# A state-space mixer and a 4-bit FFN on one core: the first group's list written anew

## The chip, the cores and the metric

The kernel runs on one core of a Trainium2 chip. The metric is the time of one execution on the device, in microseconds (us). The core has TensorE (PE; PEld is its weight load), VectorE (DVE), ScalarE (ACT), GpSimd (POOL) and SyncE (SP), which here only issues transfers. Each has its own instruction stream, in program order, and they meet through semaphores.

## The reference

Input is `u`, 16 sequences of 256 tokens with 256 features (4096 tokens). Cut to what matters:

```
zxbcdt = u @ W_in                              # z 512, x 512, B 128, C 128, dt 8
xBC = silu(causal_conv4(xBC));  dt = softplus(dt + dt_bias);  A = -exp(A_log)
Y   = ssd(x * dt, A * dt, B, C) + x * D        # per sequence, 8 heads of 64
y   = rmsnorm(Y * silu(z)) * norm_scale @ W_out
h   = layernorm(u + y)
W   = dequant(4-bit codes, scales of 32)       # gate, up: 2048 x 256; down: 256 x 2048
out = layernorm(h + (gelu(h @ Wg.T) * (h @ Wu.T)) @ Wd.T)
```

All matmuls of weights are done three times over with operands that are split into a high and a low fp32r part.

## The kernel before

**Groups.** The 4096 tokens are cut into nine groups: FIRST (number -1, 256 tokens, two tiles of 128), groups 0 to 6 (512 tokens, four tiles each) and LAST (number 7, 256 tokens). In `run(g, ...)` the mixer of group g is interleaved with the FFN of group g-1; FIRST has no FFN beside it, and its FFN runs beside the mixer of group 0. The order on every engine is a hand-written list, `SLOTS`, with names for steps: `x4`, `x5` (B and C channels), `x0` to `x3`, `z0` to `z3` (projection, convolution, silu), `CB0` (C·B products), `R0`, `R1` (decay exponents spread over 128 x 1024, ACT's part eight instructions of 128x128 into a high tile, DVE's one into a low tile), `D0`, `D1` (their prefix sums on PE, exp on ACT, product with `cb` on DVE), `XT` (transposes of x), `Y` (outputs), `g` (squares and the split of the gated output), `S` and `op` (mean square, output projection), `ln1`, `ln2` (layernorm). After the list come `uT` (split of the next group's transposed input into high, on ACT, and low, on POOL), `F1` (transposes of h into the banks `gate_bank` and `up_bank`), and `dt` and `x4` of the next group. Each step that needs a PSUM bank takes the next of four `mixer` banks by its place in `USES`.

**Weights.** The FFN's weights come as 8 packed blocks of codes (`packed`) and 24 chunks of scales. A chunk c (c%3: gate, up, down) is made in five steps: `decode(b)` on DVE (five instructions for a block of three chunks), `value(c)` on DVE (codes times scales into half of `h_res`, or into `act_sb` for odd c from 12), `upper(c)` on ACT (high part), and then for the first 12 chunks "take off" on PE (two matmuls that leave value minus high part in one of the banks `gate_bank`, `up_bank`, `down0`, `down1`) and `lower(c)` on ACT; for the others `rest(c)` on DVE. The tables `DECODE`, `VALUE`, `UPPER`, `TAKE_OFF`, `LOWER` say behind which step of the list each stands. `value(c)` waits until the take-off of chunk c-2 is done, the take-off of c for the lower part of c-4, since they share buffers.

**SP's queue.** SP issues all loads in one order, and waits in that order. Ahead of the scales of chunk c it waits until `value(c-2)` is done; ahead of the scales of chunk 3k it waits until k+1 blocks are decoded and then loads the next block; ahead of the scales of chunk 14 it does this:

```python
                if c == BESIDE_FIRST + 2:
                    load_uT(0)

                    sp.wait_ge(wt_lo.sem, BESIDE_FIRST)
                    keep_h(FIRST)
                    load_u(0)
```

`BESIDE_FIRST` is 12 and `wt_lo` counts finished lower parts. `load_uT(0)` waits for the last use of `xbc` in FIRST's `Y1`; `keep_h` copies h from `h_sb` to `h_res` once h is there; `load_u(0)` waits for that copy.

Of the kernel before, what the change touches and what calls it, by code (L numbers as in the profile page):

```python
# [13 lines left out]
P = 128  # L14
# [39 lines left out]
DECODE = {FIRST: {"x1": [2], "XT0": [3], "g0": [4]}, 0: {"x5": [5], "x1": [6], "x3": [7]}}  # L54
VALUE = {FIRST: {"x0": [2], "x1": [3], "x2": [4], "x3": [5], "D0": [6], "XT0": [7], "XT1": [8], "Y1": [9],
                 "g0": [10], "op0": [11]},
         0: {0: [12], "x0": [13], 1: [14], "z1": [15], "x2": [16], 3: [17], "z3": [18], "CB0": [19], 5: [20],
             6: [21], "XT1": [22], "D1": [23]}}
UPPER = {FIRST: {"x1": [2], "z0": [3], "z1": [4], "CB0": [5], "D1": [6], "Y0": [7], "Y1": [8], "g0": [9],
                 "op0": [10], "g1": [11]},  # L60
         0: {"x0": [12], "z0": [13], "x1": [14], 2: [15], "z2": [16], "x3": [17], 4: [18], "XT0": [19], "D0": [20],
             "Y0": [21], 7: [22], 8: [23]}}
TAKE_OFF = {"x5": [0], "x0": [1], "z0": [2], "x2": [3], "x3": [4], "D0": [5], "Y0": [6], "XT1": [7],
            "g0": [8], "op0": [9], "g1": [10], "op1": [11]}
LOWER = {FIRST: {"x1": [0], "z0": [1], "z1": [2], "x3": [3], "CB0": [4], "D1": [5], "XT1": [6], "Y1": [7],
                 "op0": [8], "g1": [9], "op1": [10], "ln1": [11]},
         0: {"z0": [12], "x1": [13], 2: [14], "z2": [15], "x3": [16], 4: [17], "XT0": [18], "D0": [19], "Y0": [20],
             7: [21], 8: [22], "XT2": [23]}}
# [49 lines left out]
def mamba_ffn_kernel(nc, u, u_t, W_in, channels, dt_bias, A_log, W_out, ffn_w, ffn_s, out):  # L118
# [42 lines left out]
    with ExitStack() as ctx:  # L161
# [60 lines left out]
        R_first = [x[:, :, :].rearrange("p k (h l) -> p (k h) l", l=P) for x in (hT_hi, hT_lo)]  # L222
# [3 lines left out]
        def R_of(g):  # L226
            return R_first if kind_of(g) == "first" else (R_hi, R_lo)
# [103 lines left out]
        def wait_R(eng, i, g):  # L331

            if i:
                wait_ready(eng, f"D{i - 1}b" if i % 2 else f"E{i // 2 - 1}", g)
            elif kind_of(g) != "first":
                wait_ready(eng, "z3", g)
            wait(eng, dA_ok, g, 1)
# [11 lines left out]
        def run(g, mixer, ffn, prep=None):  # L349


            first = kind_of(g) == "first"
# [10 lines left out]
            if not last:  # L363
# [125 lines left out]
        def _(pe):  # L489
# [18 lines left out]
            def mixer(name, g):  # L508
# [35 lines left out]
                elif kind == "D":  # L544
# [3 lines left out]
                    for n, use in enumerate((f"D{i}a", f"D{i}b")):  # L548
                        wait_bank(pe, use, g)
                        hs = slice(4 * n, 4 * n + 4)  # L550
                        upper, lower = R_of(g)
                        nc.tensor.matmul(bank(g, use)[:, :], after_r[:, :], upper[:, hs, :], start=True, stop=False)  # L552
                        nc.tensor.matmul(bank(g, use)[:, :], after_r[:, :], lower[:, hs, :], start=False,
                                         stop=True).then_inc(ready(g, use)[0].sem, 1)
                    if i % 2:
# [4 lines left out]
                        for a, rows in ((1, P), (0, HP)):  # L560
                            for n, part in enumerate(R_of(g)):
# [86 lines left out]
            def prep(g, item):  # L648
                for c in TAKE_OFF.get(item, ()) if kind_of(g) == "first" else ():
# [29 lines left out]
        def _(act):  # L679
# [134 lines left out]
            act.wait_ge(x_in.sem, 16)  # L814
            nc.scalar.activation(win_hi[:, :, X0:B0], x_raw, ACT.Copy).then_inc(win_top.sem, 1)
            upper(0)
            act.wait_ge(z_in.sem, 16)
            nc.scalar.activation(win_hi[:, :, 0:X0], z_raw, ACT.Copy).then_inc(win_top.sem, 1)
# [4 lines left out]
            upper(1)  # L823
# [4 lines left out]
        def _(dve):  # L828
# [275 lines left out]
            def prep(g, item):  # L1104
                for c in LOWER[g].get(item, ()) if kind_of(g) != "first" else ():
# [143 lines left out]
```

## Time and profile before

| | |
|---|---|
| median of 3 runs | 955.6 us (955.42 to 955.68) |
| the profiled execution's own time | 955.01 us |
| span of its trace | 953.3 us |
| PE busy | 892.7 us (94%) |
| DVE busy | 704.9 us (74%) |
| ACT busy | 532.2 us (56%) |

The span is what the trace covers; all times of single instructions below count from its start. Busy time is a union of an engine's instructions, and PE's is modelled in part. In the trace, FIRST's `F1` begins at 74.41 us and that of group 0 at 178.12 us.

### The profile page before, as it was taken

What the parts mean: (1) busy time and instruction counts of PE and PEld (TensorE: products, weight loads), DVE (VectorE), ACT (ScalarE), POOL (GpSimd) and SP (SyncE); (2) the same over time, 40 slices, a digit from 0 to 9 for tenths busy, and PEclk for the clock granted to TensorE, in tenths of its full rate; (3) what the DMA queues carried; (4) which work ended last, traced back from release to release, by engine and by line L of the source; (5) the groups of instructions that cost most, each with busy time, mean ns of one, the idle gap of its engine ahead of it and who ended that gap; (6) DMA issues with size and microseconds to landing.
All of it is one profiled execution on the core that took longest, in us unless ns stands there. A gap on an engine that the chain in (4) does not pass through costs nothing.

```text
span 953.3 us, 16507 instructions
## 1 busy us (share of the span) xinstructions
PE 892.7 (94%) x5632; PEld 773.0 (81%) x5632; DVE 704.9 (74%) x1566; ACT 532.2 (56%) x1016; POOL 72.3 (8%) x104
## 2 busy tenths in 40 slices
PE   4777789899999999999999999999999999999997
PEld 3446678788898888888888888888888888888887
DVE  6767988787769776786779876786779776867453
ACT  4743486448645775448735674547635674456232
POOL 2101000200011000200020000200020000200000
PEclk9787899999999999999999999999999999999999
DMA  4111100010002000010001000010002000100010
GB/s 135 33 58 49 32 18 12 23 45 1 1 23 67 0 0 22 22 44 0 0 22 66 0 0 22 31 35 0 0 22 67 1 1 13 45 12 1 1 35 12
DMA packets 18651, 23.13 MB, mean 24 GB/s; under 512 B 1584, under 2 KB 15152, under 8 KB 18608
## 3 DMA queue, kind: packets, MB, share of 16 engines
q1 hardware_dynamic: 18176, 22.56, 7.4%
q8 instruction: 24, 0.39, 0.2%
q14 instruction: 19, 0.16, 0.1%
q10 hardware_dynamic: 432, 0.03, 0.0%
HBM read 14.19 MB, written 4.19 MB: 19 GB/s over the span
## 4 chain that ended last, share of the span: by engine, by line
PE 78%; DVE 10%; issue 6%; POOL 3%; ACT 2%; DMA 1%; POOLq 0%; DVEq 0%; SPq 0%; ACTq 0%
PE gate_bank L493 6%; PE up_bank L493 6%; PE up_bank L495 6%; PE up_bank L494 6%; PE gate_bank L495 5%; PE gate_bank L494 5%; PE down L493 5%; PE down L495 5%; PE mixer L493 5%; PE down L494 5%; PE mixer L495 5%; PE mixer L494 5%; PE mixer L573 3%; DVE xbc L904 2%; PE mixer L552 2%
## 5 line engine op out<-in xcount | busy, mean ns | idle before, releaser
L493 PE MATMUL down<-wd_hi,in_hi 128*128 128x256 f32 x512 | 145.1, 283 | 0.7 <-DVE in_lo L1035 0.7
L495 PE MATMUL down<-wd_hi,in_lo 128*128 128x256 f32 x512 | 144.0, 281 | 0.0
L494 PE MATMUL down<-wd_lo,in_hi 128*128 128x256 f32 x512 | 143.8, 281 | 0.0
L904 DVE SCALAR_TENSOR_TENSOR xbc<-mixer,chan,xbc 128x510 f32<-128x510 f32 (+1 forms) x162 | 110.9, 685 | 27.8 <-ACT xbc L703 26.1
L760 ACT ACTIVATE in_hi<-act_sb 128x512 fp32r<-128x512 f32 (+1 forms) x144 | 83.4, 579 | 65.3 <-PE down L495 53.7
L1049 DVE SCALAR_TENSOR_TENSOR act_sb<-up_bank,act_sb 128x512 f32<-128x512 f32 (+1 forms) x144 | 90.4, 628 | 37.5 <-PE up_bank L495 18.5
L774 ACT ACTIVATE act_sb<-gate_bank 128x512 f32<-128x512 f32 (+1 forms) x144 | 79.0, 548 | 67.7 <-PE gate_bank L495 67.0
L493 PE MATMUL gate_bank<-hT_hi,wg_hi 128*128 128x512 f32 (+1 forms) x288 | 111.4, 387 | 3.1 <-DVE wg_lo L1102 3.1
L493 PE MATMUL up_bank<-hT_hi,wu_hi 128*128 128x512 f32 (+1 forms) x288 | 108.4, 376 | 6.4 <-DVE act_sb L1049 6.4
L495 PE MATMUL up_bank<-hT_hi,wu_lo 128*128 128x512 f32 (+1 forms) x288 | 107.8, 374 | 0.0
L494 PE MATMUL up_bank<-hT_lo,wu_hi 128*128 128x512 f32 (+1 forms) x288 | 107.8, 374 | 0.0
L495 PE MATMUL gate_bank<-hT_hi,wg_lo 128*128 128x512 f32 (+1 forms) x288 | 107.1, 372 | 0.0
L494 PE MATMUL gate_bank<-hT_lo,wg_hi 128*128 128x512 f32 (+1 forms) x288 | 107.0, 371 | 0.0
L1035 DVE TENSOR_TENSOR in_lo<-act_sb,in_hi 128x512 fp32r<-128x512 f32 (+1 forms) x144 | 90.0, 625 | 20.7 <-ACT in_hi L760 20.7
L493 PEld LDWEIGHTS down<-wd_hi,in_hi 128*128 128x128 f32 x512 | 97.3, 190 | 5.6 <-DVE in_lo L1035 1.1
L494 PEld LDWEIGHTS down<-wd_lo,in_hi 128*128 128x128 f32 x512 | 97.2, 190 | 4.5
L703 ACT ACTIVATE xbc<-mixer,chan 128x512 f32<-128x512 f32 (+1 forms) x54 | 39.4, 729 | 107.2 <-PE mixer L495 107.2
L495 PEld LDWEIGHTS down<-wd_hi,in_lo 128*128 128x128 f32 x512 | 97.1, 190 | 0.0
L493 PE MATMUL mixer<-uT_hi,win_hi 128*128 128x512 f32 (+1 forms) x180 | 71.2, 395 | 12.4 <-DVE wdt L1126 11.4
L1159 POOL TENSOR_TENSOR rms<-rms_v,minus_half 128x1 f32<-128x1 f32 x32 | 20.1, 628 | 741.4 <-DVE rms_v L991 741.4
L728 ACT ACTIVATE uT_hi<-tri,dA_hi 128x128 fp32r<-128x128 f32 x240 | 73.2, 391 | 0.0
L493 PEld LDWEIGHTS up_bank<-hT_hi,wu_hi 128*128 128x128 f32 x288 | 55.2, 192 | 18.3 <-DVE act_sb L1049 8.0
(200 smaller groups left out, 1936.2 us busy)
## 6 DMA issues: line engine op xcount, KB each, us to landing
xbc<-in_u_t_dram SPq DMA_DIRECT2D x7, 512.0 KB, 3.6
h_sb<-in_u_dram SPq DMA_DIRECT2D x7, 512.0 KB, 3.8
h_res<-h_sb SPq DMA_DIRECT2D x7, 512.0 KB, 2.9
out_dram<-h_res SPq DMA_DIRECT2D x7, 512.0 KB, 2.9
scales<-in_ffn_s_dram SPq DMA_DIRECT2D x24, 128.0 KB, 2.1
packed<-in_ffn_w_dram SPq DMA_DIRECT2D x8, 96.0 KB, 2.1
xbc<-in_u_t_dram SPq DMA_DIRECT2D x2, 256.0 KB, 2.8
xbc<-in_W_in_dram SPq DMA_DIRECT2D x1, 512.0 KB, 6.2
```

Source lines behind the costliest of these rows:

```text
L493: nc.tensor.matmul(dst, lh, rh, start=first, stop=False, skip_group_check=True)
L494: nc.tensor.matmul(dst, lh, rl, start=False, stop=False, skip_group_check=True)
L495: return nc.tensor.matmul(dst, ll, rh, start=False, stop=last, skip_group_check=True)
L573: mm = nc.tensor.matmul(bank(g, use)[a * HP:(a + 1) * HP, j * P:(j + 1) * P], xdt[:, h * HP:(h + 1) * HP], dec_of(g, i)[:, h, :], start=Tr ...
L703: nc.scalar.activation(xbc[:, i, 0:width(g)], bank(g, f"x{i}")[:, 0:width(g)], ACT.Identity, bias=chan[:, 24 + i:25 + i], scale=chan[:, 18 ...
L728: ins = nc.scalar.activation(R_of(g)[0][:, h, :], tri[:, :], ACT.Copy, scale=f32(dA_hi[:, i, h:h + 1]))
L760: nc.scalar.activation(in_hi[:, n % 2, 0:width(f)], act_sb[:, n % 2, 0:width(f)], ACT.Copy)\
L774: nc.scalar.activation(act_sb[:, n % 2, 0:width(f)], GB[:, 0:width(f)], ACT.Gelu_apprx_tanh, scale=CODE_SCALE).then_inc(gelu_ok.sem, 1)
L904: ins = stt(acc[:, :, d:], src[:, :, 0:SEQ - d], chan[:, c:c + 1], acc[:, :, d:], ALU.mult, ALU.add)
L1035: tt(in_lo[at], act_sb[at], f32(in_hi[at]), ALU.subtract)\
L1049: stt(inter, UB[:, 0:width(f)], CODE_SCALE, inter, ALU.mult, ALU.mult)\
L1159: tt(rms[:, i:i + 1], rms_v[:, i:i + 1], half[:, 0:1], ALU.pow).then_inc(rms_ok.sem, 1)
```

## The change

Six things change, all before the FFN of group 0 begins.

1. SP loads the B, C and dt columns of `W_in` second, ahead of the first packed block and of the x columns, and z's columns ahead of packed block 1.
2. DVE splits those columns before it decodes block 0; chunks 0 and 1 get their values later, and `x4` of FIRST starts before the x columns are split.
3. FIRST's list has `CB0` behind `x0`, `R0` behind `x1` and `R1` behind `x2`. So both R pairs exist at once, and `R1` lies in a part of `wd_hi`, `wd_lo` that is not yet filled.
4. `D` is parted: `D` is what PE and ACT do, `W` DVE's product with `cb`. `g0` stands ahead of `Y1`.
5. The tables place the chunks anew. Blocks 1 to 4 are decoded behind `z3`, `XT1`, `S1`, `ln2`. The take-offs of chunks 10 and 11 move to `x5` and `x0` of group 0, `F1` of FIRST waits for ten lower parts, not twelve, and the first `down` for eleven.
6. `uT` of group 0 stands in FIRST's list behind `S1`, and SP loads it ahead of the scales of chunk 7 instead of 14.

The full groups' order on each engine stays as it was (`W` directly behind `D`).

```diff
-    "first": [["x5", "x0", "x1", "z0", "x2", "z1", "x3", "z2", "z3", "CB0", "R0", "D0", "R1", "XT0", "D1", "Y0",
-               "XT1", "Y1", "g0", "S0", "op0", "g1", "S1", "op1", "ln1", "ln2"], []],
+    "first": [["x5", "x0", "CB0", "x1", "R0", "z0", "x2", "z1", "R1", "x3", "z2", "z3", "D0", "XT0", "D1", "W0", "W1",
+               "Y0", "XT1", "g0", "Y1", "S0", "op0", "g1", "S1", "uT", "op1", "ln1", "ln2"], []],
...
-DECODE = {FIRST: {"x1": [2], "XT0": [3], "g0": [4]}, 0: {"x5": [5], "x1": [6], "x3": [7]}}
+DECODE = {FIRST: {"z3": [1], "XT1": [2], "S1": [3], "ln2": [4]}, 0: {"x5": [5], "x1": [6], "x3": [7]}}
...
             sp.dma_start(u32[:, :, 0:HALF], uT_of(FIRST)).then_inc(uT_in.sem, 16)
+            sp.dma_start(bc_raw, win_v[:, :, B0:NIN]).then_inc(bc_in.sem, 16)
             load_block(0)
-            sp.dma_start(bc_raw, win_v[:, :, B0:NIN]).then_inc(bc_in.sem, 16)
+            sp.dma_start(x_raw, win_v[:, :, X0:B0]).then_inc(x_in.sem, 16)
             load_scales(0)
-            sp.dma_start(x_raw, win_v[:, :, X0:B0]).then_inc(x_in.sem, 16)
-            load_block(1)
             load_scales(1)
             sp.dma_start(z_raw, win_v[:, :, 0:X0]).then_inc(z_in.sem, 16)
+            load_block(1)
...
             for c in range(2, CHUNKS):
+                if c == 7:
+                    load_uT(0)
                 if c == BESIDE_FIRST + 2:
-                    load_uT(0)
...
-                        pe.wait_ge(wt_lo.sem, BESIDE_FIRST)
+                        pe.wait_ge(wt_lo.sem, BESIDE_FIRST - 2)
```

The names below are the program's tiles; `codes` and `packed` are decoding, `h_res<-codes,scales` is a `value`, `dec` and `act_sb` with `cb` are the `W` products.

SP's queue from chunk 2's scales to chunk 14's, first before, where `uT` of group 0, `keep_h` and `load_u` stand together:

```order
L415 DMA scales<-in_ffn_s_dram 128x256
L410 DMA packed<-in_ffn_w_dram 128x192
L415 DMA scales<-in_ffn_s_dram 128x256 x3
L410 DMA packed<-in_ffn_w_dram 128x192
L415 DMA scales<-in_ffn_s_dram 128x256 x2
L441 DMA xbc<-in_u_t_dram 128x2x512
L450 DMA h_res<-h_sb 128x512
L455 DMA h_sb<-in_u_dram 128x4x256
L415 DMA scales<-in_ffn_s_dram 128x256
```

and the same end of it in the changed program:

```order
L420 DMA scales<-in_ffn_s_dram 128x256
L446 DMA xbc<-in_u_t_dram 128x2x512
L420 DMA scales<-in_ffn_s_dram 128x256 x2
L415 DMA packed<-in_ffn_w_dram 128x192
L420 DMA scales<-in_ffn_s_dram 128x256 x3
L415 DMA packed<-in_ffn_w_dram 128x192
L420 DMA scales<-in_ffn_s_dram 128x256 x2
L455 DMA h_res<-h_sb 128x512
L460 DMA h_sb<-in_u_dram 128x4x256
L420 DMA scales<-in_ffn_s_dram 128x256
```

`keep_h` and `load_u` keep their place ahead of chunk 14's scales (the last row of both), and the load of `uT` has gone up.

DVE in FIRST from `z3` on, before (`cb`, `R0`, product 0, value 5, `R1`, `XT0`):

```order
L925 SCALAR_TENSOR_TENSOR zs<-zs,mixer 128x256
L931 TENSOR_TENSOR cb<-mixer,tri 128x128
L932 TENSOR_TENSOR cb<-mixer,tri 128x128
L935 TENSOR_TENSOR hT_lo<-tri,dA_lo 128x1024
L948 COPY tail<-dec 128x8
L953 TENSOR_TENSOR dec<-dec,cb 128x1024
L1094 TENSOR_TENSOR h_res<-codes,scales 128x512
L935 TENSOR_TENSOR hT_lo<-tri,dA_lo 128x1024
L940 TENSOR_TENSOR xdt<-mixer,dt_sb 128x512
```

and after, where the second row is the first of block 1's decoding and the `h_res` row is `value(3)`:

```order
L934 SCALAR_TENSOR_TENSOR zs<-zs,mixer 128x256
L1079 TENSOR_SCALAR codes<-packed 128x192
L1081 SCALAR_TENSOR_TENSOR codes<-packed,codes 128x192
L1082 TENSOR_SCALAR codes<-packed 128x192
L1084 TENSOR_SCALAR packed<-packed 128x192
L1086 TENSOR_TENSOR codes<-packed,codes 128x192
L1100 TENSOR_TENSOR h_res<-codes,scales 128x512
L949 TENSOR_TENSOR xdt<-mixer,dt_sb 128x512
L955 COPY tail<-dec 128x8
L1015 TENSOR_TENSOR xtail<-xdt,tail 128x512
L959 TENSOR_TENSOR dec<-dec,cb 128x1024
L959 TENSOR_TENSOR act_sb<-act_sb,cb 128x1024
```

`cb` and both R have moved ahead of `z3`, and between `z3` and the products stand a decoding and a value.

ACT at the start of group 0 from FIRST's first `F1` copy on, before:

```order
L767 ACTIVATE hT_hi<-gate_bank 128x256
L767 ACTIVATE hT_hi<-up_bank 128x256
L703 ACTIVATE xbc<-mixer,chan 128x512
L708 ACTIVATE dte<-dte 128x32
L703 ACTIVATE xbc<-mixer,chan 128x512
L774 ACT_TABLE_LOAD
L774 ACTIVATE act_sb<-gate_bank 128x256
L703 ACTIVATE xbc<-mixer,chan 128x512
L687 ACTIVATE y<-xbc 128x512 x2
L781 ACTIVATE wg_hi<-h_res 128x2x256
```

and after, from the convolution copy of `x5` to the lower part of chunk 11 (`wd_hi` is upper 11, `wu_lo` lower 10, `wg_hi` upper 12, `wd_lo` lower 11):

```order
L712 ACTIVATE xbc<-mixer,chan 128x512
L790 ACTIVATE wd_hi<-h_res 128x512
L794 ACTIVATE wu_lo<-down 128x2x256
L783 ACT_TABLE_LOAD
L783 ACTIVATE act_sb<-gate_bank 128x256
L712 ACTIVATE xbc<-mixer,chan 128x512
L696 ACTIVATE y<-xbc 128x512 x2
L790 ACTIVATE wg_hi<-h_res 128x2x256
L794 ACTIVATE wd_lo<-down 128x512
```

Upper 11 and lower 10 stand ahead of the table load now. The twelfth lower part, on which `keep_h` waits, has moved from FIRST to behind upper 12.

## Rows read from the trace of the kernel before

**Rows 1.** Busy time by stretch: busy (instructions) per engine, PEclk, DMA share, GB/s.

```profile
0.00:74.90 74.90, 44.92 (x208) 31.54 (x209) 53.45 (x131) 38.38 (x83) 12.90 (x26) 0.86 0.24 72
74.90:140.00 65.10, 53.23 (x312) 46.54 (x311) 55.55 (x123) 38.52 (x82) 0.00 (x0) 0.84 0.12 36
...
80.00:85.00 5.00, 5.00 (x18) 4.42 (x19) 3.41 (x7) 1.78 (x3) 0.00 (x0) 0.50 0.33 103
```

**Rows 2.** Timeline of the start: start us, us, engine, line, operation [idle before <-releaser].

```profile
1.81 0.43 SPq L419 DMA_DIRECT2D y<-in_W_in_dram  x1
...
7.39 0.63 ACT L812 ACTIVATE win_hi<-y 128x512 fp32r<-128x512 f32 x1 [2.79 <-DMA y<-in_W_in_dram]
...
10.35 0.68 DVE L1123 TENSOR_TENSOR win_lo<-y,win_hi 128x512 fp32r<-128x512 f32 x1
...
11.38 0.55 PE L493 MATMUL mixer<-uT_hi,win_hi 128*128 128x256 f32 x1 [11.38 <-DVE wdt L1126]
```

**Rows 3.** Timeline of DVE: the silus of `x4`, `x5` in FIRST; a decoding's first row, the row behind.

```profile
22.30 0.75 DVE L839 SCALAR_TENSOR_TENSOR xbc<-y,xbc 128x256 f32<-128x256 f32 x2
...
47.81 0.25 DVE L1073 TENSOR_SCALAR codes<-packed 128x192 int32<-128x192 int32 x1
...
49.23 1.22 DVE L953 TENSOR_TENSOR act_sb<-act_sb,cb 128x1024 f32<-128x1024 f32 x1
```

**Rows 4.** Timeline of ACT in FIRST: W_out's scaling, and `R0`.

```profile
23.14 1.69 ACT L800 ACTIVATE zs<-zs,chan 128x256 f32<-128x256 f32 x4
...
37.57 2.43 ACT L728 ACTIVATE hT_hi<-tri,dA_hi 128x128 fp32r<-128x128 f32 x8
```

**Rows 5.** The page: transfers, KB each, median us from issue to landing.

```profile
h_sb<-in_u_dram SPq DMA_DIRECT2D x7, 512.0 KB, 3.8
...
scales<-in_ffn_s_dram SPq DMA_DIRECT2D x24, 128.0 KB, 2.1
...
h_res<-h_sb SPq DMA_DIRECT2D x2, 256.0 KB, 3.2
...
y<-in_W_in_dram SPq DMA_DIRECT2D x1, 264.0 KB, 5.6
```

**Rows 6.** Timeline of PE: a take-off and the next one, and FIRST's `F1`.

```profile
62.94 1.91 PE L655 MATMUL up_bank<-h_res,ident 128*128 128x512 f32 x2
...
65.07 1.06 PE L655 MATMUL down<-h_res,ident 128*128 128x512 f32 x2
...
74.41 0.50 PE L626 MATMUL gate_bank<-ident,h_sb 128*128 128x128 f32 x2 [4.14 <-DVE h_sb L1029]
```

**Rows 7.** Timeline of DVE: the normalization of h at FIRST's end, and that line over the run.

```profile
71.80 2.54 DVE L1029 TENSOR_SCALAR h_sb<-h_sb,mv,lnr 128x256 f32<-128x256 f32 x2 [1.16 <-POOL lnr L1148]
...
L1029 DVE TENSOR_SCALAR h_sb<-h_sb,mv,lnr x32: 401/408/1354, 71.8 to 893.7; 128x256 f32<-128x256 f32 x32
```

**Rows 8.** Timeline, PE and DVE: `x4` of group 1, and DVE's first step on its dt.

```profile
181.17 0.41 PE L493 MATMUL mixer<-uT_hi,win_hi 128*128 128x512 f32 x1
...
184.46 0.19 DVE L855 TENSOR_TENSOR dtx<-mixer,dtb 128x32 f32<-128x32 f32 x1 [1.29 <-PE mixer L504]
```

**Rows 9.** Timeline of DVE in group 0: dt, `x5`'s convolution, value 12, value 14.

```profile
80.66 0.19 DVE L855 TENSOR_TENSOR dtx<-mixer,dtb 128x32 f32<-128x32 f32 x1 [4.55 <-PE mixer L504]
...
84.31 2.31 DVE L904 SCALAR_TENSOR_TENSOR xbc<-mixer,chan,xbc 128x510 f32<-128x510 f32 x3 [0.79 <-ACT xbc L703]
...
88.42 0.68 DVE L1094 TENSOR_TENSOR h_res<-codes,scales 128x512 f32<-128x512 fp8e4 x1
...
95.21 0.68 DVE L1094 TENSOR_TENSOR h_res<-codes,scales 128x512 f32<-128x512 fp8e4 x1
```

**Rows 10.** Timeline of SP's queue: `keep_h`, `load_u`, and the scales of chunk 14.

```profile
74.43 0.53 SPq L450 DMA_DIRECT2D h_res<-h_sb  x1
78.67 0.39 SPq L455 DMA_DIRECT2D h_sb<-in_u_dram  x1
89.13 0.34 SPq L415 DMA_DIRECT2D scales<-in_ffn_s_dram  x1
```

More of the change, by code:

```diff
@@ L38 @@
 SLOTS = {
[3 rows of a table removed]
[3 rows of a table added]
              ["S3", "op3", "ln1"], ["ln2"]],
[4 rows of a table removed]
[4 rows of a table added]
+             [], [], []]}
 BESIDE_FIRST = 12
-DECODE = {FIRST: {"x1": [2], "XT0": [3], "g0": [4]}, 0: {"x5": [5], "x1": [6], "x3": [7]}}
-VALUE = {FIRST: {"x0": [2], "x1": [3], "x2": [4], "x3": [5], "D0": [6], "XT0": [7], "XT1": [8], "Y1": [9],
-                 "g0": [10], "op0": [11]},
+DECODE = {FIRST: {"z3": [1], "XT1": [2], "S1": [3], "ln2": [4]}, 0: {"x5": [5], "x1": [6], "x3": [7]}}
+VALUE = {FIRST: {"x0": [1], "x2": [2], "D0": [3], "W1": [4], "g0": [5], "Y1": [6], "op0": [7], "g1": [8], "op1": [9],
+                 "ln1": [10], "ln2": [11]},
@@ L57 @@
          0: {0: [12], "x0": [13], 1: [14], "z1": [15], "x2": [16], 3: [17], "z3": [18], "CB0": [19], 5: [20],
[L58 to L68, printed above, removed]
+             6: [21], "XT1": [22], "W1": [23]}}
+UPPER = {FIRST: {"CB0": [1], "z1": [2], "D1": [3], "Y0": [4], "g0": [5], "g1": [6, 7], "S1": [8], "ln1": [9],
+                 "ln2": [10]},
+         0: {"x5": [11], "x0": [12], "z0": [13], "x1": [14], 2: [15], "z2": [16], "x3": [17], 4: [18], "XT0": [19],
+             "D0": [20], "Y0": [21], 7: [22], 8: [23]}}
@@ new lines @@
+TAKE_OFF = {FIRST: {"x5": [0], "x1": [1], "x3": [2], "W1": [3], "XT1": [4], "Y1": [5], "S1": [6], "op1": [7, 8],
+                    "ln1": [9]},
+            0: {"x5": [10], "x0": [11]}}
+LOWER = {FIRST: {"x0": [0], "z0": [1], "z2": [2], "g0": [3], "Y1": [4], "op0": [5], "op1": [6, 7], "ln1": [8],
+                 "ln2": [9]},
+         0: {"x5": [10], "x0": [11]}}
+REST = {"z0": [12], "x1": [13], 2: [14], "z2": [15], "x3": [16], 4: [17], "XT0": [18], "W0": [19], "Y0": [20],
+        7: [21], 8: [22], "XT2": [23]}
@@ L220, in mamba_ffn_kernel, with R_of @@
         wout_raw = zs[:, :, HALF:]
-        R_first = [x[:, :, :].rearrange("p k (h l) -> p (k h) l", l=P) for x in (hT_hi, hT_lo)]
+        R_first = [[x.rearrange("p k (h l) -> p (k h) l", l=P) for x in pair]
+                   for pair in ((hT_hi[:, :, :], hT_lo[:, :, :]), (wd_hi[:, 12:16, :], wd_lo[:, 12:16, :]))]
         dec_first = act_sb[:, :, :].rearrange("p k (h l) -> p (k h) l", l=P)
         minus_i = in_hi[:, 0, HALF:HALF + P]
-        def R_of(g):
-            return R_first if kind_of(g) == "first" else (R_hi, R_lo)
+        def R_of(g, i):
+            return R_first[i] if kind_of(g) == "first" else (R_hi, R_lo)
         def dec_of(g, i):
@@ L331, in wait_R @@
         def wait_R(eng, i, g):
[L333 to L336, printed above, removed]
+            if kind_of(g) != "first":
+                wait_ready(eng, f"D{i - 1}b" if i % 2 else f"E{i // 2 - 1}" if i else "z3", g)
             wait(eng, dA_ok, g, 1)
@@ L362, in run @@
             last = kind_of(g) == "last"
-            if not last:
+            if not first and not last:
                 mixer("uT", g + 1)
@@ L550, in mixer @@
                         hs = slice(4 * n, 4 * n + 4)
-                        upper, lower = R_of(g)
+                        upper, lower = R_of(g, i)
                         nc.tensor.matmul(bank(g, use)[:, :], after_r[:, :], upper[:, hs, :], start=True, stop=False)
@@ L560, in mixer @@
                         for a, rows in ((1, P), (0, HP)):
-                            for n, part in enumerate(R_of(g)):
+                            for n, part in enumerate(R_of(g, i)):
                                 mm = nc.tensor.matmul(bank(g, use)[0:rows, :],
@@ L648, in prep @@
             def prep(g, item):
-                for c in TAKE_OFF.get(item, ()) if kind_of(g) == "first" else ():
+                for c in TAKE_OFF[g].get(item, ()):
                     b = chunk_bank(c)
@@ L727, in mixer @@
                     for h in range(H):
-                        ins = nc.scalar.activation(R_of(g)[0][:, h, :], tri[:, :], ACT.Copy,
+                        ins = nc.scalar.activation(R_of(g, i)[0][:, h, :], tri[:, :], ACT.Copy,
                                                    scale=f32(dA_hi[:, i, h:h + 1]))
@@ L790, in prep @@
                     upper(c)
-                for c in LOWER[g].get(item, ()) if kind_of(g) == "first" else ():
+                for c in LOWER[g].get(item, ()):
                     lower(c)
@@ L796, in any_mixer @@
                 mixer(name, g)
+                if name == "x5" and kind_of(g) == "first":
+                    upper(0)
+                    act.wait_ge(z_in.sem, 16)
+                    nc.scalar.activation(win_hi[:, :, 0:X0], z_raw, ACT.Copy).then_inc(win_top.sem, 1)
                 if name == "x1" and kind_of(g) == "first":
@@ L813, in _ @@
             nc.scalar.activation(wdt[:, :, 0, :], bc_raw[:, :, DT0 - B0:], ACT.Copy).then_inc(win_top.sem, 1)
[L814 to L818, printed above, removed]
             act.wait_ge(small_in.sem, 16 * 2)
@@ L822, in _ @@
             mixer("x4", FIRST)
-            upper(1)
+            act.wait_ge(x_in.sem, 16)
+            nc.scalar.activation(win_hi[:, :, X0:B0], x_raw, ACT.Copy).then_inc(win_top.sem, 1)
             run_all(act, any_mixer, ffn, prep)
@@ L941, in mixer @@
                        dt_sb[:, i, :].unsqueeze(2).to_broadcast([P, H, HP]), ALU.mult).then_inc(x_ok.sem, 1)
-                    if kind_of(g) == "first" and i == 0:
-                        x_tail(i, g)
-                elif kind == "D":
+                elif kind == "W":
                     d = dec_of(g, i)
@@ L1104, in prep @@
             def prep(g, item):
-                for c in LOWER[g].get(item, ()) if kind_of(g) != "first" else ():
+                for c in REST.get(item, ()) if kind_of(g) != "first" else ():
                     rest(c)
@@ L1135, in _ @@
             mixer("x4", FIRST)
+            value(0)
+            dve.wait_ge(win_top.sem, 3)
+            tt(win_lo[:, :, X0:B0], x_raw, f32(win_hi[:, :, X0:B0]), ALU.subtract).then_inc(win_ok.sem, 1)
             run_all(dve, mixer, ffn, prep)
```

18 lines of the change are left out of this document (8 added, 10 removed), and 12 rows, old and new, of tables (SLOTS, USES).

## The prediction

> **What bounds the kernel now.** I read the busy time by stretch first. From 140 us on PE is the bound: of the page's 892.7 us the two first stretches hold 98.2 [rows 1], so the other 813 us of the span hold 794.6 of them, 98%. The change touches nothing there, so the time can only change by the moment at which PE comes to its dense part. Ahead of it lie FIRST (to 74.41 us, PE busy 44.9 of 74.9) and the first half of group 0, where DVE is busy 55.6 of 65.1 us and PE 53.2 [rows 1]. The timeline of DVE shows where that half has slack: 4.55 us before dt, 0.79 before `x5`'s convolution [rows 9], then almost none until 122 us. So a microsecond by which DVE is late between 90 and 122 us is a microsecond of the whole, and one by which it gets its dt earlier is one too. Two numbers decide: when FIRST's `F1` begins (74.41 [rows 6]), and how long DVE then takes to its dense part and through it.
>
> **FIRST, step by step.** Times are from the span's start; instructions whose rows are not shown are priced by the same timelines, at their distance from start to start.
>
> The B, C columns were issued at 1.81 and used at 7.39, a landing of 5.6 us [rows 2, 5]. They are issued 0.5 earlier and have no packed block ahead: I take 6.7 us, with 4.5 (a landing like the 3.2 us of a 256 KB copy [rows 5]) and 6.9 as bounds. From the landing PE's first matmul follows after 0.7 (ACT's copy 0.63) plus 1.03 (10.35 to 11.38, the two DVE splits [rows 2]), since value 0, value 1 and their scales no longer stand ahead. That is 8.4 instead of 11.38, 3.0 earlier.
>
> Of this most goes again. The silus of `x4` and `x5` began 10.9 us after PE's first matmul (11.38 to 22.30 [rows 2, 3]); now value 0 (0.6) and the x split (1.1) stand inside, and the silus take 0.75: 21.8. PE has `CB0` behind `x0` and waits for them, and behind it stands `x1`. PE has then been idle for some 4 us, and after such an idle (4.14 us before 74.41 [rows 6]) the granted clock was 0.50, the 1.2 GHz level, in 80 to 85 us [rows 1]; at that level `CB0` and `x1` cost 1.4 and 1.3: 24.5 instead of 20.2. From there ACT leads: copy and tanh (0.8), W_out (1.7 [rows 4] and 1.0), `R0` 2.4 [rows 4], z0's tanh, lower 1, `x2`'s copy (1.3): DVE's convolution of `x2` at 32.0, which began at 29.7. DVE's convolution, silu and value 2 (2.5), ACT's upper 2, `R1`, copy of `x3` (3.5): 38.0. Convolution, silus and z of `x3` (2.9): 40.9, where before z3 ended at 37.4. But `cb` and both R are made by then. They cost DVE 3.74 us of waiting for exp alone before.
>
> Decoding block 1 costs 1.4 (47.81 to 49.23 [rows 3]): 42.3. Here is a new wait: SP loads block 2 only when block 1 is decoded, and chunk 3's scales behind it, while `value(3)` is DVE's next instruction. Issue 0.4 and a landing of 2.1 to 2.3 [rows 5] make it 44.9 to 45.1. I found nothing that hides it; the transposed x and both products queue behind it. From 45.1 DVE's list runs to the end of `Y1` without a wait that I can find, 13.9 us: 59.0 (58.2 before). `g0` is then done, decoding 2 too.
>
> Next, `value(8)` waits for take-off 6, which stands behind `S1` on PE. `S1` can start at 63.5; a take-off costs 2.1 at the low level (62.94 to 65.07 [rows 6]) and 1.2 at the high one: `value(8)` at 64.7 to 66.0. Decoding 3 ends some 2.2 later, and chunk 9's scales wait behind packed block 4 as above: 2.5. Values 9, statistics and the power on POOL cost 2.9. The normalization itself gets cheaper: 2.54 us for two instructions beside POOL's split of `uT`, which is now done long before, against a median of 0.41 each otherwise [rows 7]: 0.8 for both, 1.8 saved. `F1` comes at 73.2 (takes at the high level) to 74.5; I take 74.0. The ten lower parts that it waits for are there by then. **First term: -0.4 us** (-2.4 to +0.5).
>
> **Group 0, the clock.** PE works almost without a gap from `S1` (63.5) on: take-offs 6 to 9 and `op1`, and waits under 2 us before `F1`, not 4.14 [rows 6]. With the low level (0.50 [rows 1]) `F1` to DVE's dt took 6.25 us (74.41 to 80.66 [rows 6, 9]); `x4` of group 1 to dt took 3.3 (181.17 to 184.46 [rows 8]), with `F1` 3.7. DVE is free 2.7 us after `F1` (value 11, decoding 4, split of h stand there now, hidden by its wait). So up to 2.5 from the first wait and 0.79 from the second [rows 9], 3.3 in all; in this group a gap of 1.9 us was followed by 3.4 us at the low level, which leaves 1.6; nothing if PE stays low. **Second term: -2.3 us** (-3.3 to 0). The two take-offs that moved here, ACT's three instructions (1.5 us) and the table load behind lower 10 are hidden: PE idles 12 us of this half and ACT 26 [rows 1], and DVE reaches the first product only after decoding 5.
>
> **Group 0, SP's queue.** `keep_h` was issued at 74.43, as soon as h was there, `load_u` 4.24 later, and chunk 14's scales at 89.13 when `value(12)` was done [rows 10]; `value(14)` did not wait for them. Now `keep_h` waits for the twelfth lower part, which ACT does behind upper 12, so behind `value(12)`: 1.1 after its end (upper and lower), up to 2.5 if the tanhs are late. From `value(12)`'s end (89.0) to `value(14)` (95.2) were 6.2 us [rows 9]. Against them stand 1.1 to 2.5, the copy, 4.24 [rows 10] or the 3.2 of its row [rows 5], 0.4 for `load_u`, and the scales' landing: 2.1 alone, up to 3.9 behind 512 KB that land in 3.8 [rows 5]. That is 6.8 to 11.0; `value(14)` waits for 0.6 to 4.8 us. I take 2.5: the copy between its prices, the scales between theirs, ACT on time. Queued behind `value(14)` are `x1`'s convolution and all of DVE, and behind upper 14 on ACT the gelu of unit 2, so PE's unit 3. DVE has no slack to give it back. **Third term: +2.5 us** (+0.6 to +4.8).
>
> The Trainium skill bears on this term ("DMA: Bandwidth & Descriptors", section "Anatomy of one DMA"): about 2.0 us fixed plus the bytes at 436 GB/s. By it the 256 KB copy would take 2.6 us and the scales 2.3, and the third term would be near +0.2, the sum 2.5 us below 955.6. Its copy and the trace's, 4.24, differ.
>
> **Sum.** -0.4 - 2.3 + 2.5 = -0.2 us on the profiled execution's 955.01, which lies 0.6 below the median: 955.4 for the median.
>
> **Rivals.** What can be told from no change is 0.2%, 1.9 us: below 953.7 or above 957.5.
>
> *The queue costs nothing* (0.16). Copy and scales land quickly, and `value(14)` waits 0.6. For it: the median of the two 256 KB copies, 3.2 [rows 5]. Against: 4.24 at this very place. -0.4 - 2.3 + 0.6 = -2.1: 953.5.
>
> The Trainium skill's rule above is the same case with 953.1.
>
> *B and C land early* (0.10), at 4.5: the chain of FIRST keeps 2.2 more. For it: nothing stands ahead but `uT`. Against: 5.6 us for rows of 1056 B. 953.2.
>
> *FIRST's waits are overrated* (0.07): high clock at its end and ACT's chain shorter. About 953.
>
> *PE stays at the low level into group 0* (0.13). The gap before `F1` or before `S1` drops it. For it: in 74 to 85 us it stayed low for over 10 us [rows 1, 6]. The second term is gone: 957.7. It decides once less than 0.2 us of the 2.3 are left.
>
> *The queue at its upper price* (0.13): 4.24, scales behind `load_u`, tanhs late, 4.8: 957.7.
>
> *The change does nothing* (0.03): all is absorbed before 122 us, 955.6. With my own forecast (0.38) this is the case of no change.
>
> **Numbers.** Faster 0.33 (0.16 + 0.10 + 0.07), same 0.41, slower 0.26. My own case ranges over 953.8 to 957.4. The range takes in the rivals of both sides and, since they can meet, a little beyond each: 952.0 to 958.7.
>
> **What would show it.** Right: PE's first matmul near 8.4; DVE waits some 2.5 us on scales before `value(3)` and again before `value(9)`; h's normalization 0.4 each; `F1` between 73 and 75; dt of group 0 3.7 to 5.5 us behind `F1`; SP issues `keep_h` some 16 us behind `F1`, and DVE waits for scales before `value(14)`. Wrong: `F1` below 72 or above 76; no wait before `value(14)`; a wait in group 0 that I don't name, above all of ACT behind lower 10.

## Result: 0.4% slower, outside the range

The changed kernel takes 959.27 us (median of 5, 957.37 to 961.87) against 955.6 for the kernel before in the same series, a ratio of 1.004 (95% interval 1.0022 to 1.0057). The forecast was 955.4, in a range up to 958.7. Sent again with the experiments it gave 959.47, ratio 1.0047 (1.0033 to 1.006). The execution profiled first is the fastest of its five, 957.37, with a span of 955.7; the later one took 959.74, span 957.9. Both are used, since they differ in FIRST.

The start of the changed kernel, by the timeline (columns as in [rows 2]):

```profile
1.31 0.46 SPq L423 DMA_DIRECT2D y<-in_W_in_dram  x1
...
5.82 0.63 ACT L825 ACTIVATE win_hi<-y 128x512 fp32r<-128x512 f32 x1 [1.27 <-DMA y<-in_W_in_dram]
...
7.51 0.55 PE L499 MATMUL mixer<-uT_hi,win_hi 128*128 128x256 f32 x1 [7.51 <-DVE wdt L1129]
```

The columns land in 4.5 us instead of 5.6, and PE begins 3.9 us sooner than in [rows 2]. Then DVE's timeline of the changed kernel, in order: values 3, 8 and 9, the normalization of h, dt of group 0, `x5`'s convolution, values 12 and 14.

```profile
45.52 0.69 DVE L1100 TENSOR_TENSOR h_res<-codes,scales 128x512 f32<-128x512 fp8e4 x1 [3.05 <-DMA scales<-in_ffn_s_dram]
...
66.38 0.69 DVE L1100 TENSOR_TENSOR h_res<-codes,scales 128x512 f32<-128x512 fp8e4 x1 [1.83 <-PE down L666]
...
71.16 0.69 DVE L1100 TENSOR_TENSOR h_res<-codes,scales 128x512 f32<-128x512 fp8e4 x1 [2.00 <-DMA scales<-in_ffn_s_dram]
...
74.38 0.74 DVE L1035 TENSOR_SCALAR h_sb<-h_sb,mv,lnr 128x256 f32<-128x256 f32 x2 [0.95 <-POOL lnr L1152]
...
82.11 0.19 DVE L864 TENSOR_TENSOR dtx<-mixer,dtb 128x32 f32<-128x32 f32 x1 [4.30 <-PE mixer L510]
...
85.75 2.31 DVE L913 SCALAR_TENSOR_TENSOR xbc<-mixer,chan,xbc 128x510 f32<-128x510 f32 x3 [0.79 <-ACT xbc L712]
...
89.86 0.68 DVE L1100 TENSOR_TENSOR h_res<-codes,scales 128x512 f32<-128x512 fp8e4 x1
...
98.49 0.69 DVE L1100 TENSOR_TENSOR h_res<-codes,scales 128x512 f32<-128x512 fp8e4 x1 [1.75 <-issue]
```

The brackets are the reading. The two waits for scales in FIRST stand where the queue was said to make them. But dt still waits 4.30 us for PE and `x5` 0.79, as in [rows 9]. FIRST's `F1` on PE, and SP's queue, in the changed kernel (to [rows 6, 10]):

```profile
75.18 0.70 PE L635 MATMUL gate_bank<-ident,h_sb 128*128 128x128 f32 x2 [1.92 <-DVE h_sb L1035]
...
91.92 0.53 SPq L455 DMA_DIRECT2D h_res<-h_sb  x1
94.27 0.39 SPq L460 DMA_DIRECT2D h_sb<-in_u_dram  x1
94.71 0.50 SPq L420 DMA_DIRECT2D scales<-in_ffn_s_dram  x1
```

And its clock (busy time by stretch; the number behind POOL's is the granted clock):

```profile
75.00:80.00 5.00, 4.82 (x18) 4.34 (x19) 2.70 (x9) 0.77 (x2) 0.00 (x0) 0.51 0.26 74
80.00:85.00 5.00, 5.00 (x17) 4.29 (x16) 2.73 (x6) 1.13 (x3) 0.00 (x0) 0.50 0.00 2
85.00:90.00 5.00, 5.00 (x25) 3.51 (x24) 4.04 (x10) 4.37 (x7) 0.00 (x0) 0.96 0.00 0
```

With these the loss splits up. `F1` begins 0.77 later (75.18 to 74.41). From `F1` to dt are 6.93 us, not 6.25: +0.68. From dt to value 14 are 16.38, not 14.55: +1.83. That is 3.28 at value 14, and the next `F1`, group 0's, comes 3.25 later (181.37 to 178.12): nothing is given back on the way. The span grew by 2.4, so about 0.9 came back in the dense part, where the clock is 1.00 instead of 0.98 from 800 to 900 us. In the second profile `F1` comes at 76.44, 2.0 late, and value 14 is 4.64 late; its clock from 60 to 70 us is 0.66, where the first has 0.83. From 800 to 900 us it has 0.98, and there nothing comes back: its span is 4.6 longer.

### The profile page after: what moved, and what is told of

The parts are those of the page before. It is cut to its first block, busy times and chain, and to the rows that moved or that the text cites. A ratio compares the mean times of both kernels' runs of the same rounds, so it can differ in the third digit from the quotient of the medians.

```text
span 955.7 us, 16504 instructions
## 1 busy us (share of the span) xinstructions
PE 892.9 (93%) x5632; PEld 772.7 (81%) x5632; DVE 701.2 (73%) x1566; ACT 532.3 (56%) x1016; POOL 72.8 (8%) x104
## 4 chain that ended last, share of the span: by engine, by line
PE 76%; DVE 11%; issue 6%; ACT 3%; POOL 3%; DMA 2%; SPq 0%; POOLq 0%; DVEq 0%; ACTq 0%
PE gate_bank L499 6%; PE up_bank L499 6%; PE up_bank L500 6%; PE up_bank L501 6%; PE gate_bank L501 5%; PE gate_bank L500 5%; PE down L499 5%; PE down L501 5%; PE down L500 5%; PE mixer L499 5%; PE mixer L501 4%; PE mixer L500 4%; PE mixer L579 3%; DVE xbc L913 2%; PE mixer L547 1%
```

## Experiments

Theory: three separate waits make the loss, (a) value 3's for scales behind a late decoding, (b) the clock after `F1`, (c) `keep_h` and `load_u` ahead of chunk 14's scales. Rivals: they stand behind one another, so that mending one gains nothing; or the clock falls whatever PE does before `F1`. Each kernel starts from the changed one unless said otherwise. The first four ran together; "against again" compares medians with `again`.

**again**, unchanged.

> The changed kernel once more, nothing edited. It shows how far its runs lie apart (five of them lay between 957.4 and 961.9 us, those of the kernel before within 0.8) and whether the parts of the loss seen in the first profile come back. If the spread is TensorE's clock, a slower execution shows a stretch at the low level that the first profile does not have, at the end of the first group or in group 0, and the waits of VectorE keep their size.

959.47: the reference for the rest. In its profile the waits of values 3 and 9, dt and `x5` keep their size within 0.1 us, and value 14's is 1.93. What grows is value 7's wait for scales (0.72 to 1.15) and, more, value 8's for PE (1.83 to 2.58), at the longer low level of FIRST's end. So the clock makes the larger part of the 1.3 us by which `F1` differs between the two profiles.

**keep_later**, for (c).

```diff
-                if c == BESIDE_FIRST + 2:
+                if c == BESIDE_FIRST + 4:
```

> SP does the copy of h and the load of the next u two chunks later (ahead of chunk 16's scales, not chunk 14's). Theory queue: VectorE's wait of 1.75 us before value 14 goes, nothing takes its place, and the time falls by 1.8 us, to about 957.5 where the unedited one gives 959.3. Rival theory (the wait only fills slack): the wait goes and the time stays within 0.5 us, because value 14's followers wait for ScalarE or TensorE then.

957.99 (957.09 to 959.02), ratio 1.0026: -1.5 against again. SP and DVE of this kernel:

```profile
95.57 0.33 SPq L420 DMA_DIRECT2D scales<-in_ffn_s_dram  x1
96.01 0.53 SPq L455 DMA_DIRECT2D h_res<-h_sb  x1
97.43 0.69 DVE L1100 TENSOR_TENSOR h_res<-codes,scales 128x512 f32<-128x512 fp8e4 x1
```

Value 14 has no bracket: there is no wait. From dt (82.87) to it are 14.56 us, as in the kernel before (14.55). So what the third term measured was all SP's queue.

**dec1_early**, for (a): block 1 is decoded behind `R0`.

```diff
-DECODE = {FIRST: {"z3": [1], "XT1": [2], "S1": [3], "ln2": [4]}, ...
+DECODE = {FIRST: {"R0": [1], "XT1": [2], "S1": [3], "ln2": [4]}, ...
```

> Block 1 is decoded behind R0 on VectorE, in its 2.5 us wait for z0's tanh, not behind z3, so SP can load block 2 and chunk 3's scales some 10 us earlier. Theory FIRST's own waits: the decoding (1.4 us) and the wait before value 3 (3.05 us) both leave the path, TensorE's transposes of h begin about 4 us sooner, and the time falls by 3 to 4.5 us. Rival: exp on ScalarE and the second product's wait take most of it, the gain is 1 to 2 us.

955.22 (954.6 to 958.34), ratio 1.0007 (0.9997 to 1.0017): -4.2. In this kernel value 3 comes at 40.99 and does not wait, value 4, behind both products, at 45.34, where the changed kernel has value 3, and `F1` comes at 71.39, 5.0 us sooner than in `again` and 3.8 than in the first profile:

```profile
40.99 0.68 DVE L1100 TENSOR_TENSOR h_res<-codes,scales 128x512 f32<-128x512 fp8e4 x1
...
43.07 1.22 DVE L959 TENSOR_TENSOR dec<-dec,cb 128x1024 f32<-128x1024 f32 x1
44.21 1.22 DVE L959 TENSOR_TENSOR act_sb<-act_sb,cb 128x1024 f32<-128x1024 f32 x1
45.34 0.68 DVE L1100 TENSOR_TENSOR h_res<-codes,scales 128x512 f32<-128x512 fp8e4 x1
```

One entry of the table thus costs as much as the whole change lost. The wait was in my sum, but only as time; I did not ask what the change would be without it.

**fill_clock**, for (b): six matmuls on data that is there, into a free bank, between take-off 9 and `F1`.

```diff
+                    if c == 9:
+                        pe.wait_ge(wt_lo.sem, 8)
+                        for _ in range(6):
+                            nc.tensor.matmul(OB[1][:, :], minus_i, prep_dst(0)[0], start=True, stop=True,
+                                             skip_group_check=True)
```

> Six extra matmuls (their result is overwritten and not used) behind take-off 9 keep TensorE busy for 1.3 of the 1.9 us before it transposes h. Theory clock: the fall to 1.2 GHz around 75 us comes from that gap, so the projections of group 0 run at 2.4 GHz for all or most of the 8 us, VectorE gets dt 1.5 to 3 us sooner after the transposes, and the time falls by 1.5 to 3 us. Rival: the lower level is not decided by that gap; the granted clock falls all the same within a few us and the time stays within 0.5 us.

955.55 (954.4 to 959.14), ratio 1.001 (0.9999 to 1.0021): -3.9. Clock, `F1` and dt of this kernel:

```profile
75.00:80.00 5.00, 4.61 (x30) 4.21 (x31) 3.60 (x14) 1.51 (x4) 0.00 (x0) 1.00 0.24 68
80.00:85.00 5.00, 5.00 (x28) 3.84 (x26) 4.75 (x8) 4.01 (x7) 0.00 (x0) 1.00 0.02 8
```

```profile
75.39 0.51 PE L635 MATMUL gate_bank<-ident,h_sb 128*128 128x128 f32 x2 [0.54 <-DVE h_sb L1040]
...
79.25 0.19 DVE L869 TENSOR_TENSOR dtx<-mixer,dtb 128x32 f32<-128x32 f32 x1 [1.23 <-PE mixer L510]
```

`F1` to dt is 3.86 now instead of 6.93 (my 3.7 for the high level), DVE waits 1.23 instead of 4.30, `x5`'s wait is gone, and value 14 comes at 94.66 instead of 98.49. So the clock after `F1` costs 3.8 us at value 14, 3.1 of it ahead of dt, and filling the rest ahead of `F1` keeps it.

**fill_half**: three matmuls in place of six.

```diff
-                        for _ in range(6):
+                        for _ in range(3):
```

> The changed kernel with three extra matmuls behind take-off 9, where the filling above has six: TensorE then rests about 1.2 us ahead of F1 of FIRST, against 1.92 in the changed kernel and 0.54 with six. My prediction took it that a shorter rest lets the clock stay up. If the clock after F1 goes by degrees with the rest, dt of group 0 comes between the two, about 1.5 us sooner, and the time is about 957.5. If 1.2 us is as bad as 1.92, it is 959.5 and the granted clock is 0.50 from 76 to 85; if it is as good as 0.54, 955.5 and 1.00.

956.15 (953.66 to 959.28), ratio 1.0012 (1.0 to 1.0024): near -3.3 by the ratios.

```profile
76.75 0.50 PE L635 MATMUL gate_bank<-ident,h_sb 128*128 128x128 f32 x2 [1.21 <-DVE h_sb L1040]
```

After this rest of 1.21 us the clock is 1.00 from 75 to 90 us. In these traces a rest ahead of FIRST's `F1` had one of two ends, not degrees: 1.00 after 0.54 and 1.21 us, 0.50 after 1.92 and 4.14.

**before_fill**: the kernel before with fourteen such matmuls behind take-off 11, nothing of the change.

```diff
+                    if c == 11:
+                        pe.wait_ge(wt_lo.sem, 11)
+                        for _ in range(14):
+                            nc.tensor.matmul(OB[0][:, :], minus_i, prep_dst(0)[0], start=True, stop=True,
+                                             skip_group_check=True)
```

> The kernel before with fourteen extra matmuls behind take-off 11, on data that is there and into a free bank, which keep TensorE busy until F1 of FIRST; nothing of the change. If the lower clock of group 0's first ten microseconds comes of the wait ahead of F1 and costs the kernel before as much as the changed one, dt of group 0 comes about 3 us sooner and the time falls to 952.3 (951.5 to 953.2). If the clock is lost for another reason than that wait (the light projection work itself), the granted clock stays at one half between 76 and 85 us and the time at 955.6.

951.72 (951.14 to 953.22), ratio 0.9965 (0.9952 to 0.9977). The clock is 1.00 from 75 to 90 us, and dt comes at 77.83 instead of 80.66, with `F1` 0.45 sooner (73.96): 3.87 us from one to the other, not 6.25. So the cost of the clock is no effect of the change: both kernels pay it, and I had credited the change with removing it.

**dec13_keep**: `dec1_early` and `keep_later` in one, and block 3 decoded behind `op0` instead of `S1`.

```diff
-DECODE = {FIRST: {"z3": [1], "XT1": [2], "S1": [3], "ln2": [4]}, ...
+DECODE = {FIRST: {"R0": [1], "XT1": [2], "op0": [3], "ln2": [4]}, ...
...
-                if c == BESIDE_FIRST + 2:
+                if c == BESIDE_FIRST + 4:
```

> The changed kernel with three places of its tables moved: block 1 decoded behind R0 instead of z3, block 3 behind op0 instead of S1, and keep_h with load_u two chunks later in SP's queue. No filling. Alone, the first gave -4.3 us and the last -1.5. The second lets SP send the scales of chunk 9 about 1.4 us sooner: value 9 waits 2.1 us for them in the changed kernel, so up to 1.4 us sooner at F1. If the three waits are independent the time is 955.2 - 1.5 - 1 = 952.5 (951.5 to 954.0). If the three stand behind one another, so that the next wait takes up what one gives back, it stays at 954.5 to 955.5.

955.48 (951.77 to 957.2), ratio 0.9989 (0.9975 to 1.0002): my 952.5 missed. Value 9 waits for PE instead of scales, and `F1` comes at 71.98, no sooner than in `dec1_early`: the third move gains nothing. The time is the one that the expectation has for waits that stand behind one another (954.5 to 955.5), but not by that way: `F1` of group 0 comes at 175.56, 2.5 us sooner than in `dec1_early` (178.06), so the queue's gain is there. The rest of the miss lies later. This `F1` is 2.6 us sooner than in the kernel before, but the next one at 286.71, 2.0 later than its 284.74: 111.2 us between them, against 106.6. The clock around `F1` of group 0, in the kernel before and then in this one:

```profile
175.00:180.00 5.00, 1.89 (x9) 1.89 (x10) 3.48 (x6) 0.95 (x2) 2.59 (x2) 0.78 0.00 0
180.00:185.00 5.00, 5.00 (x32) 4.65 (x32) 3.44 (x11) 1.91 (x3) 0.89 (x2) 0.88 0.01 2
```

```profile
175.00:180.00 5.00, 4.44 (x19) 4.15 (x19) 3.29 (x9) 1.20 (x2) 0.04 (x1) 0.50 0.00 0
180.00:185.00 5.00, 5.00 (x21) 4.64 (x20) 0.95 (x6) 1.85 (x2) 0.90 (x2) 0.50 0.01 2
185.00:190.00 5.00, 5.00 (x16) 3.93 (x15) 4.74 (x10) 2.91 (x5) 0.00 (x0) 0.66 0.14 50
```

PE waits the same 3.56 us ahead of this `F1` in both. What follows differs in length.

**all_four**: the three moves and the diff of `fill_clock`, nothing else.

> The last kernel with six extra matmuls behind take-off 9 that keep TensorE busy until F1 of FIRST. The filling alone gave -3.9 us. If the clock after F1 is a cost of its own, this stands 2.5 to 4 us under the kernel with the three moves: 949.5 (948.5 to 951.5), below the kernel before by 0.6%. If after the earlier F1 group 0 waits for something else (x5's copy, scales 14), it gives under 1.5 us more.

949.87 (949.25 to 951.7), ratio 0.9948 (0.9934 to 0.9962), as expected. `F1` comes at 72.29, dt at 76.15, `F1` of group 0 at 172.79.

**fill_two_gaps**: in addition fourteen matmuls ahead of `F1` of group 0.

```diff
+                    if isinstance(f, int) and f == 0:
+                        wait(pe, gelu_ok, FIRST, NF)
+                        for _ in range(14):
+                            nc.tensor.matmul(GB[:, :], wg_hi[:, 0, 0:P], wg_hi[:, 0, 0:512], start=True, stop=True,
+                                             skip_group_check=True)
                     wait(pe, h_ok, f, tiles(f))
```

> The kernel with the three moves and the filling ahead of F1 of FIRST, plus fourteen extra matmuls into the free gate bank ahead of F1 of group 0, where TensorE waits 3.56 us in every trace. Traces so far differ in what follows that wait: the granted clock falls for 2 to 15 us (0.50 from 175 to 188 in the kernel with the three moves, 0.78 to 0.88 from 175 to 185 in the kernel before) and group 0 then lasts 111.2 us instead of 106.6. If the wait is the cause, as ahead of F1 of FIRST, group 0 lasts about 105.5 us, the time is 948.7 (948.0 to 949.6) and the spread of the runs shrinks. If the fall is not tied to that wait, the time stays at 949.9.

947.85 (946.84 to 949.23), ratio 0.9917 (0.9902 to 0.9932). The clock is 1.00 from 165 to 195 us and from this `F1` to the next are 105.3 us (173.67 to 279.00). That is a gain of 3.0 us by the ratios, more than expected. The spread of the runs, which was to shrink, did not: 2.4 us, and 2.5 in `all_four`.

**fill_three_gaps**: in addition twelve into `OB[0]` ahead of `S1` of FIRST.

```diff
+                    if i and kind_of(g) == "first":
+                        pe.wait_ge(wt_lo.sem, 3)
+                        for _ in range(12):
+                            nc.tensor.matmul(OB[0][:, :], minus_i, prep_dst(0)[0], start=True, stop=True,
+                                             skip_group_check=True)
                     wait(pe, sq_sum, g, i + 1)
```

> The last kernel plus twelve extra matmuls ahead of S1 of FIRST, where TensorE waits 4.3 to 6 us and then does the second output projection at 0.41 us a product instead of 0.28. If the clock rises there too, take-offs 6 and 7 and op1 end some 1 to 1.5 us sooner and the time is 947.5 (946.7 to 948.7). The rival: twelve at the lower clock last 5.1 us, and where the wait is shorter they push S1 back, so that nothing is won: 948.7 or more.

946.5 (944.92 to 947.95), ratio 0.9908 (0.9893 to 0.9924), the fastest kernel of the study, 0.9% under the kernel before. The clock is 1.00 from 40 to 90 us, and `F1` comes at 70.07 instead of 72.68. Its interval overlaps that of two gaps; the traces tell them apart, the times hardly.

**uT_late**: `uT` split behind `ln2` again.

```diff
-               "Y0", "XT1", "g0", "Y1", "S0", "op0", "g1", "S1", "uT", "op1", "ln1", "ln2"], []],
+               "Y0", "XT1", "g0", "Y1", "S0", "op0", "g1", "S1", "op1", "ln1", "ln2"], []],
...
-            if not first and not last:
+            if not last:
```

> The changed kernel with uT of group 0 split behind ln2 again, its load left early: the two GpSimd subtractions stand beside the normalization again. My step says that the two normalization operations then take about 1.2 us each instead of 0.4 and F1 comes 0.8 to 1.8 us later, so 960.3 to 961.3 against 959.5. The rival: the operations take 0.37 us as now, since GpSimd's work is only displaced, and the time stays at 959.0 to 959.8.

963.67 (962.07 to 964.28), ratio 1.0085 (1.0072 to 1.0099): +3.6 by the ratios, twice what I expected, and by another way. Normalization, `x4`'s first matmul and two steps of the decoding in this kernel:

```profile
76.13 0.73 DVE L1035 TENSOR_SCALAR h_sb<-h_sb,mv,lnr 128x256 f32<-128x256 f32 x2 [0.94 <-POOL lnr L1152]
...
77.67 1.30 DVE L1081 SCALAR_TENSOR_TENSOR codes<-packed,codes 128x192 int32<-128x192 int32 x1
78.90 1.31 DVE L1082 TENSOR_SCALAR codes<-packed 128x192 int32<-128x192 int32 x1
```

```profile
80.15 0.79 PE L499 MATMUL mixer<-uT_hi,win_hi 128*128 128x512 f32 x1 [2.10 <-POOL uT_lo L1159]
```

POOL's subtractions (3.16 us from 76.93) fall behind the normalization, which keeps its 0.73. They do stretch what DVE does beside them: the decoding steps take 1.30 and 1.31, elsewhere 0.36 and 0.25. The cost is PE's second rest, 2.10 us, while it waits for `uT_lo`, and a dt 9.4 us behind `F1`. So the early split is worth 3.6 us by being ready when `F1` is done, not by sparing the normalization, as my first term had it: with the split behind `ln2` again that costs 0.73, as in the changed kernel (0.74).

**undo_bc**: packed block 0 loaded ahead of the B, C columns again.

```diff
+            load_block(0)
             sp.dma_start(bc_raw, win_v[:, :, B0:NIN]).then_inc(bc_in.sem, 16)
-            load_block(0)
```

> The changed kernel with packed block 0 loaded ahead of the B, C and dt columns again. In the changed kernel those columns landed about 2.9 us sooner than before, and PE's first matmul came 3.9 us sooner, but SP's scales of chunk 3 still end the wait at 45.5 us. If the early columns are worth what they moved at the start, this is 1.5 to 3 us slower than the changed kernel, 961 to 962.5. If the gain is swallowed by that later wait for scales, which hangs on the decoding behind z3, it is under 0.5 us: 959.0 to 960.0. I expect the first, since the decoding that releases the load stands behind the convolution stage and moves with it.

962.75 (961.95 to 964.54), ratio 1.0079 (1.0063 to 1.0095): +3.1 by the ratios. The expectation had a wrong number: the columns are used 1.6 us sooner than before (5.82 to 7.39), not 2.9.

```profile
8.22 0.63 ACT L825 ACTIVATE win_hi<-y 128x512 fp32r<-128x512 f32 x1 [3.67 <-DMA y<-in_W_in_dram]
...
9.92 0.55 PE L499 MATMUL mixer<-uT_hi,win_hi 128*128 128x256 f32 x1 [9.92 <-DVE wdt L1129]
```

PE begins 2.4 us later than in the changed kernel and `F1` comes at 79.64, 3.2 behind `again`: in these traces what the start gains is passed on whole, and some more.

## Why the prediction was wrong

**The step that failed** is the second term, "Group 0, the clock": "PE works almost without a gap from `S1` (63.5) on", so that it would be at the high level in group 0, -2.3 us. It measured +0.68. The wait was as forecast, under 2 us, and PE was at the high level before it (take-off 9 at 71.90 took 1.12). But it rested 1.09 us ahead of take-off 9 and 1.92 ahead of `F1`, and then stood at the low level for some 10 us, as in the kernel before. The level even fell sooner: in [rows 6] `F1`'s first pair took 0.50, here 0.70. That the kernel before pays for it too is shown by `before_fill`; that filling the rest keeps the level, by `fill_clock` and `fill_half`. The price was up to 3.3 by my working; at value 14 `fill_clock` has 3.8.

The prediction had a row against its own choice: the gap of 1.9 us in group 0 of the kernel before, which was followed by 3.4 us at the low level. These are the first matmul behind it and the clock of its stretch:

```profile
94.71 0.36 PE L493 MATMUL gate_bank<-hT_hi,wg_hi 128*128 128x256 f32 x1 [1.89 <-DVE wg_lo L1102]
```

```profile
95.00:100.00 5.00, 5.00 (x25) 4.58 (x24) 4.96 (x13) 2.45 (x6) 0.00 (x0) 0.66 0.09 28
```

A rest as long as the forecast one had lost the level there. I took 3.4 us of it as the worse case, and the level stayed low three times as long. I had the mechanism as the rival "PE stays at the low level into group 0", with 957.7 and a chance of 0.13, and that chance was too small.

**The first term**, -0.4, measured +0.77, and +2.0 in the second profile. The milestones held at first: `x2`'s convolution 32.01 (32.0), `x3`'s 38.07 (38.0), value 3 at 45.52 (45.1), the normalization 1.8 us cheaper. In part that was luck: PE began at 7.51 and not at 8.4, and by the end of the silus of `x4` and `x5` (21.80, forecast 21.8) these 0.9 us were gone. So the rival "B and C land early" had a part of its condition (used at 5.82, between 6.7 and 4.5) and brought nothing that can be seen there. `Y1` was 0.9 late, half of it a wait of 0.42 for PE behind the products that I had not found. Value 8, at 66.38, is past my later bound of 66.0, which has take-off 6 at the low level: so it ran, and `S1` was 0.6 late. My 74.0 lay between the two levels; both profiles have the low one there. In `fill_three_gaps`, where the level is high, `F1` comes 2.6 us sooner (70.07 to 72.68).

**The third term**, +2.5, measured +1.83, and `keep_later` shows that it is the queue alone. Within it ACT was 1.4 behind value 12, and the copy took 2.35, not 4.24 [rows 10]. In `before_fill`, the same place of the same queue, it took 2.36. So 4.24 was one slow sample; what made it slow is not shown. The scales took 3.8 behind 512 KB, near the upper price. Against the forecast the three terms are off by +1.2, +3.0 and -0.7 us in the first profile, so the third one's error hid a part of the others'.

The Trainium skill ("DMA: Bandwidth & Descriptors", section "Anatomy of one DMA — SWDGE (gpsimd) path") gives its rule for transfers that GpSimd issues, which my prediction did not say. Here SP issues them. The rule makes 2.6 for this copy and 2.3 for the scales, both estimates; the traces have 2.35 and 3.8, so it comes near for the copy and not for a transfer behind another.

**The median** lies 1.9 above the profiled execution, before only 0.6. The second profile shows where: FIRST's end at the low level for longer.

**The range** was too narrow on the slow side. It stopped at one rival at a time beyond my own case, although the clock and the first term hang on the same level of TensorE's clock and so fail together: 957.7 with +0.8 to +2.0 in place of -0.4 is 959 to 960.

## What to carry to other kernels

When an engine is credited with a faster state, find a row in which it kept that state across a rest as long as the one that is forecast; without one, the state of the old trace is the likelier, and a row in which it lost the state counts for more than a shorter wait. Where a queue makes a new wait, price the change once with that wait and once with the step that releases it moved: here one table entry was worth 4.2 us. Price a transfer from several samples of its place, not one. And where an engine rests just ahead of a stretch that it limits, a few matmuls without use are worth a try: one such filling gave 0.35% on the kernel before, whose PE is 94% busy, and a second 0.3% more on the changed one.

## What was unexpected of the hardware

The length of the rest alone does not tell what the clock does. A rest of 1.92 us ahead of `F1` lost it (0.50 for some 10 us), one of 1.21 did not. But in `fill_three_gaps` PE rested 2.91 us ahead of `S1`, behind the twelve matmuls of the filling, and the stretches behind it are at 1.00:

```profile
61.15 0.38 PE L601 MATMUL mixer<-tri,y 128*128 128x1 f32 x2 [2.91 <-DVE y L999]
```

And after the same 3.56 us ahead of group 0's `F1` the stretches above give some 3 us at the low level in the kernel before and 13 in `dec13_keep` (the shortfall of the granted clock by twice the stretch). The Trainium skill ("TensorE: Matmul & The Clock Gate", section "Part 1: The HAM clock gate (the "warmup" mystery)") says, of the slow matmuls at a kernel's start, that their number varies from run to run of one kernel. The traces here, in the middle of a kernel and of two kernels, would fit that.

It would also explain the spread of `dec13_keep`, 951.8 to 957.2, and the mean granted clock of each of its runs speaks for it: 0.977 to 0.979 in the three fastest (951.8 to 952.8), 0.971 to 0.974 in the six slowest (955.8 to 957.2). A difference of 0.006 over the span is an estimated 11 us more at the low level, about the 10 by which the two kernels above differ. Only one run of it has a profile, so it is not shown that the other runs differ at this place. The fillings remove the rests and the low stretches with them, 3.0 us at group 0's `F1` alone.
